# Local attention layers: table products from PSUM, own buffers for rotated q and k, feed-forward per batch, new order

## The chip, the core and the metric

The kernel runs on one core of a Trainium2 chip. A core has TensorE (PE: matmuls and transposes, results into PSUM), VectorE (DVE), ScalarE (ACT: activation functions, copies out of PSUM), GpSimd (POOL: elementwise work on SBUF) and SyncE (SP: here it starts the DMA transfers). They run side by side, each through its own instructions in their written order, and wait for each other on semaphores. The metric is the device time of one execution in microseconds (us); lower is better.

## What is computed

x has 8 batches of 256 tokens of 128 numbers. It passes a state space block, a cross attention block and six layers of local attention with feed-forward; after each of the three comes x = layernorm(x + block(x)). Only the six layers matter here. For one layer (16 heads of 64 numbers, windows of 32 tokens, 341 hidden numbers):

```python
def attn_layer(x, Wqkv, qs, ksc, Wo):
    q, k, v = split(x @ Wqkv)                  # per head
    q, k = l2norm(q) * qs, l2norm(k) * ksc
    q = q * cos * scale + rotate_half(q) * sin * scale
    k = k * cos / scale + rotate_half(k) * sin / scale
    # each window of 32 queries sees its own and the previous 32 keys
    attn = softmax(where(mask, -inf, q @ k.T * 8))
    return (attn @ v) @ Wo

def ffn_layer(x, g, bln, W1, b1, W2, b2):
    a, gate = split((layernorm(x) * g + bln) @ W1 + b1)
    return a * gelu(gate) @ W2 + b2

for i in range(6):
    x = attn_layer(shift_tokens(x), ...) + x
    x = ffn_layer(shift_tokens(x), ...) + x
```

shift_tokens moves the upper 64 columns down by one token.

## The kernel before

Three blocks follow each other: state_space_block, cross_attention_block, window_layers. Only window_layers (and the packing of its weights) is touched. The whole x lies in SBUF (xall, 16 tiles of 128 tokens by 128). A batch is two tiles, t = 0 and 1. There are ITERS = 6 x 8 = 48 iterations i (layer i // 8, batch i % 8), and two slots in each. The loop over i is the same on every engine; the order inside a slot is written out by hand in a function slot(i, t, stages) of each engine. A slot works on up to four tiles at once, in four stages:

- A, unit u: the token tile is transposed (transpose_tokens, L1314, in the slot before), six projections of 512 columns (project, L1399) go through the two PSUM banks psA: four for q and k, two for v. ScalarE copies the first four to qkraw (L1125) and squares them (L1162). VectorE multiplies qkraw with the cosine and sine tables into m12 (L1250, one product of 128x2048 each for q and k) and sums the squares (L1268). GpSimd makes the scaled table (L1054), adds the two halves in place in m12 (rotate, L1035) and multiplies with 1/norm into qkr (scale, L1041). ScalarE copies v (L1110); SyncE moves it into V96.
- B, the unit before (v): q and k are transposed (L1393, into psA again) and copied (L1132), then for two groups g of 8 heads: scores (L1344 for the mask, L1350), maximum and subtraction (L1220, L1225), exponentials (L1118), denominators (L1229, L1231), normalisation on GpSimd (L1029), transposes of the probabilities (L1362), copies (L1101) and the product with v (times_v, L1383; group 1 one slot later). psS, psP and psO are one buffer each.
- C, the unit before that (wu): the output projection (L1453), the residual x1 (L1263), the shift of x1 into xsC by DMA (L986, L987), layer norm statistics (L1271, L1274), the normalised tile hatC (L1284). GpSimd adds the bias b2 to x1 (x1b, L1070).
- D, the unit three back (du), one tile a slot: hatC is transposed (L1410), scaled (xnT, L1143), multiplied with both halves of W1 (w1, L1424, tokens in the rows, 341 columns each), the bias added (L1240), GELU (L1165, with a table load before it and one after it, L1166), the product a x gelu on GpSimd (hh, L1062), three transposes (L1467), two copies (hT, L1177 and L1178), the product with W2 (L1484) and the residual addition into xall (L1288).

ScalarE holds one table set of functions at a time: GELU is in another than exponential and logarithm. The weights of a layer (f_W) come in eight shares, one per iteration, all sizes packed by column (W_QKV, W_O, W_1, ...), L1009. The helper weights_here waits for the share that holds a column; A_full[n] and A_free[n] mark the fills of psA: 0 to 3 for q and k, 4 to 7 for their transposes, 8 and 9 for v.

## Time and profile before

| what | value |
|---|---|
| median of 3 runs | 2977.41 us (2975.38 to 2978.07) |
| the profiled execution, its own time | 2978.97 us |
| its span (first to last instruction) | 2977.2 us |
| mean granted TensorE clock | 0.977 |
| busy, share of the span: TensorE | 2639.6 us, 89% |
| VectorE | 2064.9 us, 69% |
| ScalarE | 1929.3 us, 65% |
| GpSimd | 1649.6 us, 55% |
| window layers, first to last L1054 | 831.8 to 2896.9 us |

A share of the span is an average over all three blocks. What one slot of the window layers costs is read from a stretch of the trace: the busy times of one slot, TensorE's rows in order of time, and the chain of work, which goes back from the last instruction to what released it, step by step. A matmul row's end overlaps the start of the next, so the distance of two starts tells the cost, not the duration.

### The profile page before, as it was taken

How to read it: one execution, taken by the hardware profiler on the slowest of the kernel's cores; microseconds unless marked ns; L12 is line 12 of the kernel's file. 1: busy time of each engine (PE TensorE's matmuls, PEld its weight loads, DVE VectorE, ACT ScalarE, POOL GpSimd, SP SyncE). 2: the span in 40 equal slices, each digit the busy share in tenths (PEclk: the TensorE clock that was granted, in tenths of full speed). 3: DMA queues.
4: the chain of work that ended last, by engine and by line, in shares of the span. 5: the costliest groups of instructions: out<-in, count | busy, mean ns of one | idle time of the engine just before them, and what ended most of it. 6: DMA issues, size and time to landing. Idle time of an engine off the chain costs nothing.

```text
span 2977.2 us, 64423 instructions
## 1 busy us (share of the span) xinstructions
PE 2639.6 (89%) x23097; PEld 1760.7 (59%) x23097; DVE 2064.9 (69%) x3311; ACT 1929.3 (65%) x3411; POOL 1649.6 (55%) x1188
## 2 busy tenths in 40 slices
PE   5787788999979999999999999999999999999995
PEld 2343345777746666666666666666666666666664
DVE  6898995555556767677676777767677676767764
ACT  3233232333357778787777878777787877778784
POOL 1342441000047777676777767677776777767672
PEclk9998999999989999999999999999999999999997
DMA  2000001000011121212112121211212121121211
GB/s 100 1 0 0 1 0 47 0 0 0 0 34 47 41 54 46 56 39 56 46 39 56 46 56 39 56 46 39 56 46 56 39 54 48 39 56 46 54 41 33
DMA packets 86713, 112.65 MB, mean 38 GB/s; under 512 B 60944, under 2 KB 62096, under 8 KB 85904
## 3 DMA queue, kind: packets, MB, share of 16 engines
q1 hardware_dynamic: 86672, 112.20, 14.3%
q8 instruction: 14, 0.23, 0.0%
q14 instruction: 27, 0.22, 0.0%
HBM read 29.28 MB, written 1.05 MB: 10 GB/s over the span
## 4 chain that ended last, share of the span: by engine, by line
ACT 26%; DVE 13%; POOL 12%; PE 9%; issue 5%; DMA 5%; SPq 1%; POOLq 0%; DVEq 0%; ACTq 0%
POOL f_qkr L1041 10%; ACT f_sq L1162 6%; DVE f_den L1229 5%; DMA f_xsC<-f_x 4%; ACT L1165 4%; ACT L1166 3%; ACT f_qT L1132 3%; ACT f_kT L1132 3%; DVE f_ssq L1268 3%; ACT f_Pr L1118 3%; PE f_psA L1399 2%; POOL f_Pr L1029 2%; PE f_psA L1393 2%; PE f_psO L1383 2%; ACT f_oT L1114 2%
## 5 line engine op out<-in xcount | busy, mean ns | idle before, releaser
L1035 POOL TENSOR_TENSOR f_m<-f_m 128x1024 f32<-128x1024 f32 x192 | 637.8, 3342 | 241.9 <-DVE f_m L1250 241.9
L1250 DVE TENSOR_TENSOR f_m<-f_qkraw,f_tab 128x2048 f32<-128x2048 f32 x192 | 433.5, 2299 | 480.7 <-POOL f_tab L1054 470.7
L1399 PE MATMUL f_psA<-f_W,f_xT 128*128 (+1 forms) x1152 | 605.8, 622 | 12.9 <-issue 8.1
L1029 POOL TENSOR_TENSOR f_Pr<-f_Pr,f_rden 128x384 f32<-128x384 f32 x384 | 310.1, 828 | 372.3 <-DVE f_rden L1231 372.3
L1041 POOL TENSOR_TENSOR f_qkr<-f_m,f_rn 128x1024 f32<-128x1024 f32 x192 | 361.0, 1901 | 0.9 <-DVE f_rn L1281 0.9
L208 POOL TENSOR_TENSOR m_HC<-m_Hs,m_Ct 128x512 f32<-128x512 f32 x128 | 163.8, 1279 | 299.6 <-DVE m_Hs L349 299.6
L1362 PE MATMUL f_psP<-ident,f_Pr 128*96 128x128 f32 x1536 | 238.1, 278 | 100.6 <-POOL f_Pr L1029 65.8
L1362 PEld LDWEIGHTS f_psP<-ident,f_Pr 128*96 128x96 f32 x1536 | 156.4, 127 | 267.8 <-POOL f_Pr L1029 149.6
L1125 ACT ACTIVATE f_qkraw<-f_psA 128x512 f32<-128x512 f32 x384 | 228.7, 596 | 110.0 <-PE f_psA L1399 110.0
L1101 ACT ACTIVATE f_PT<-f_psP 96x512 f32<-96x512 f32 x384 | 228.5, 595 | 84.4 <-PE f_psP L1362 79.3
L1383 PEld LDWEIGHTS f_psO<-f_PT,f_V 96*64 96x64 f32 x6144 | 217.7, 138 | 100.9 <-issue 89.3
L1054 POOL TENSOR_TENSOR f_tab<-f_base_tab,f_W 128x256 f32<-128x256 f32 x96 | 69.8, 727 | 368.0 <-DVE f_maskb L1215 368.0
L1383 PE MATMUL f_psO<-f_PT,f_V 96*64 96x64 f32 x6144 | 257.6, 230 | 0.0
L1229 DVE TENSOR_REDUCE f_den<-f_Pr 128x8 f32<-128x768 f32 x192 | 179.8, 937 | 107.5 <-ACT f_Pr L1118 107.3
L1350 PE MATMUL f_psS<-f_kT,f_qT 64*64 64x96 f32 x6144 | 244.0, 249 | 0.0
L1350 PEld LDWEIGHTS f_psS<-f_kT,f_qT 64*64 64x64 f32 x6144 | 207.8, 133 | 60.9 <-issue 60.9
L1399 PEld LDWEIGHTS f_psA<-f_W,f_xT 128*128 128x128 f32 x1152 | 181.7, 191 | 96.8 <-issue 61.8
L263 ACT ACTIVATE m_psD<-m_psD,m_negA 128x512 f32<-128x512 f32 x128 | 84.7, 662 | 227.1 <-PE m_psD L423 227.1
L1268 DVE TENSOR_REDUCE f_ssq<-f_sq 128x32 f32<-128x2048 f32 x96 | 218.5, 2276 | 0.0
L1453 PEld LDWEIGHTS f_psO<-f_W,f_oT 128*128 128x128 f32 x1536 | 187.8, 193 | 45.5 <-issue 45.4
L1393 PE MATMUL f_psA<-ident,f_qkr 128*128 128x128 f32 x1536 | 206.8, 278 | 7.3 <-POOL f_qkr L1041 1.5
L1393 PEld LDWEIGHTS f_psA<-ident,f_qkr 128*128 128x128 f32 x1536 | 173.6, 142 | 45.5 <-ACT f_qT L1132 20.9
(172 smaller groups left out, 5160.1 us busy)
## 6 DMA issues: line engine op xcount, KB each, us to landing
f_V<-f_Vt SPq DMA_DIRECT2D x96, 384.0 KB, 4.3
f_V<-f_Vt SPq DMA_DIRECT2D x96, 256.0 KB, 3.6
f_W<-in_f_W SPq DMA_DIRECT2D x48, 381.5 KB, 3.8
f_V<-f_Vt SPq DMA_DIRECT2D x48, 128.0 KB, 4.6
f_xsA<-xall SPq DMA_DIRECT2D x97, 32.0 KB
f_xsA<-xall SPq DMA_DIRECT2D x97, 31.8 KB
f_xsC<-f_x SPq DMA_DIRECT2D x96, 32.0 KB
f_xsC<-f_x SPq DMA_DIRECT2D x96, 31.8 KB
```

Source lines behind the costliest of these rows:

```text
L1029: pool.tensor_tensor(pv, pv, rv.unsqueeze(3).broadcast_to([P, 2, 2, KEYS]), ALU.mult).then_inc(Pr_ready[g][j], 1)
L1035: pool.tensor_tensor(mv[:, 0], mv[:, 0], mv[:, 1, :, ::-1, :], ALU.add).then_inc(rot_done[j], 1)
L1041: pool.tensor_tensor(qkr[:, j * INNER:(j + 1) * INNER].rearrange("p (h d) -> p h d", d=DH), m12[:, j, 0, :].rearrange("p (h d) -> p h d", ...
L1125: act.activation(qkraw[:, n * 512:(n + 1) * 512], psA[n % 2][:, :], ACT.Copy).then_inc(A_free[n], 1)
L1229: dve.tensor_reduce(den[:, g, :], Pr[:, g, :, :], axis=AX.X, op=ALU.add).then_inc(den_done[g], 1)
L1250: dve.tensor_tensor(m12[:, j, :, :].rearrange("p m (h d) -> p m h d", d=DH), rv.unsqueeze(1).broadcast_to([P, 2, H, DH]), tab[:, t, j, :, ...
L1268: dve.tensor_reduce(ssq[:, :], sq[:, :].rearrange("p (h d) -> p h d", d=DH), axis=AX.X, op=ALU.add).then_inc(ssq_ready, 1)
L1350: ins = pe.matmul(S4[half * HQ:(half + 1) * HQ, par, c, :], qT[r, q, 4 * g + c, k0:k0 + HQ], kT[r, q, 4 * g + c, k0:k0 + KEYS], start=Fals ...
L1362: ins = pe.transpose(psP[0:KEYS, n, :], Pr[:, g, (h % 2) * 4 + h // 2, :], ident[:, :])
L1383: ins = pe.matmul(psO[(h % 2) * DH:(h % 2) * DH + DH, h // 2, half * HQ:(half + 1) * HQ], V96[:, tile, half, hh_ * DH:(hh_ + 1) * DH], PT[ ...
L1393: ins = pe.transpose(p[:, c * P:(c + 1) * P], qkr[:, col:col + P], ident[:, :])
L1399: pe.matmul(psA[n % 2][:, :], xT[:, t, :], weights(i, W_QKV + n * 512, 512), start=True, stop=True).then_inc(A_full[n_fill], 1)
```

## The change

- The table products read the projections from PSUM, four of 128x1024 instead of two of 128x2048 (table_products). Each frees its bank. The squares are taken from PSUM too, 512 columns at a time (square). qkraw goes. The sum of squares stands right behind the products.
- rotate writes into qkr, which now has a buffer for each t, as two instructions of 512 for each of q and k; scale works in place there. The table of a slot is made in the slot before (scaled_tables).
- The feed-forward runs once per batch, over both tiles (256 tokens): stage D in slots with t = 0 and stage E in slots with t = 1. hatC of both tiles is transposed into xnT (256 columns), W1 is the stationary operand and comes as its own transfer f_W1 into its own buffer (once per iteration, waiting for h01_ready and h2_ready), its bias a column. So the hidden numbers lie in the partitions, in three pieces (FC = 128, 128, 85), GELU takes the bias from its own instruction, the gated product is one VectorE instruction a piece (gated), and no transposes, hidden copies or bias additions remain. Table loads for GELU come once per two slots. w2 runs for both tiles in E.
- x1 + b2 goes straight into xall; the residual addition takes both tiles at once.
- The order on every engine is new: see the slots below. times_v alternates between the two heads of a pair.

```diff
@@ GpSimd @@
+            def rotate(u, t, j):
+                pool.wait_ge(A_free[2 * j + 1], u + 1)
+                at_least(pool, A_full[7], u - 1)
                 mv = m12[:, j, :, :].rearrange("p m (h two d) -> p m h two d", two=2, d=DH // 2)
-                pool.tensor_tensor(mv[:, 0], mv[:, 0], mv[:, 1, :, ::-1, :], ALU.add).then_inc(rot_done[j], 1)
+                qv = qkr[:, t, j * INNER:(j + 1) * INNER].rearrange("p (h two d) -> p h two d", two=2, d=DH // 2)
+                pool.tensor_tensor(qv[:, :, 0, :], mv[:, 0, :, 0, :], mv[:, 1, :, 1, :], ALU.add)
+                pool.tensor_tensor(qv[:, :, 1, :], mv[:, 0, :, 1, :], mv[:, 1, :, 0, :], ALU.add).then_inc(rot_done[j], 1)
...
                 if "A" in stages:
+                    rotate(u, t, 0)
+                    rotate(u, t, 1)
+                    scaled_tables(u + 1, i + t, 1 - t)
...
@@ ScalarE @@
-                    act.activation(qkraw[:, n * 512:(n + 1) * 512], psA[n % 2][:, :], ACT.Copy).then_inc(A_free[n], 1)
+                    act.activation(sq[:, n * 512:(n + 1) * 512], psA[n % 2][:, :], ACT.Square).then_inc(squared[n], 1)
...
                 if "A" in stages:
+                    square(0)
+                if "D" in stages:
...
+                    act.activation(xnT[:, :], psD[0][:, 0:T2], ACT.Identity, bias=weights(i - 2, W_LN + 1, 1), scale=weights(i - 2, W_LN, 1)).then_inc(xnT_ready, 1)
+                if "A" in stages:
+                    square(1)
                 if "C" in stages:
                     evacuate_probs(1, 0)
...
                 if "C" in stages:
                     evacuate_out(1)
                 if "B" in stages:
+                    evacuate_qk(1)
+                if "D" in stages:
+                    at_least(act, h01_ready, (i - 2) * 2)
+                    at_least(act, h2_ready, i - 2)
+                    for c in range(3):
+                        src, j = bank_of(c)
+                        if c != 1:
+                            act.wait_ge(gate_full[j], i - 1)
+                        act.activation(ge[0:FC[c], c, :], src[0:FC[c], :], ACT.Gelu, bias=bias_col(3 + c)[0:FC[c], :]).then_inc(ge_ready, 1)
+                    act.preload_act_table_set(LN_EXP)
+                if "B" in stages:
                     evacuate_qk(2)
                     evacuate_qk(3)
-                if "A" in stages:
-                    act.wait_ge(A_free[3], u + 1)
-                    act.activation(sq[:, :], qkraw[:, :], ACT.Square).then_inc(sq_ready, 1)
...
                     exponentials(0)
...
+                    evacuate_tokens(u + 1, 1 - t)
+                    evacuate_v(0)
+                if "B" in stages:
+                    evacuate_probs(0, 0)
+                    exponentials(1)
+                    evacuate_probs(0, 1)
...
+                if "A" in stages:
+                    evacuate_v(1)
                 if "B" in stages:
                     evacuate_out(0)
@@ VectorE @@
+                def gated(c):
+                    src, j = bank_of(c)
+                    if c != 1:
+                        dve.wait_ge(a_full[j], i - 1)
+                    dve.scalar_tensor_tensor(out=hT[0:FC[c], c, :], in0=src[0:FC[c], :], scalar=bias_col(c)[0:FC[c], :],
+                                             in1=ge[0:FC[c], c, :], op0=ALU.add, op1=ALU.mult).then_inc((h01_ready, h01_ready, h2_ready)[c], 1)
+                def table_products(n):
+                    j = n // 2
...
+                    dve.wait_ge(squared[n], u + 1)
+                    half = slice((n % 2) * 512, (n % 2) * 512 + 512)
+                    dve.tensor_tensor(m12[:, j, :, half].rearrange("p m (h d) -> p m h d", d=DH),
+                                      psA[n % 2][:, :].rearrange("p (h d) -> p h d", d=DH).unsqueeze(1).broadcast_to([P, 2, H // 2, DH]),
+                                      tab[:, t, j, :, :].unsqueeze(2).broadcast_to([P, 2, H // 2, DH]), ALU.mult).then_inc(A_free[n], 1)
...
+                    for n in range(4):
+                        table_products(n)
+                    dve.wait_ge(squared[3], u + 1)
+                    dve.tensor_reduce(ssq[:, :], sq[:, :].rearrange("p (h d) -> p h d", d=DH), axis=AX.X, op=ALU.add).then_inc(ssq_ready, 1)
+                if "E" in stages:
+                    dve.wait_ge(ge_ready, (i - 1) * 3)
+                    gated(2)
                 if "B" in stages:
                     less_maximum(v, 0)
...
+                if "E" in stages:
+                    gated(0)
+                    gated(1)
...
                 if "B" in stages:
                     denominators(v, 1)
+                if "E" in stages:
+                    dve.wait_ge(w2_full, i - 1)
+                    dve.wait_ge(x1b_ready, (i - 1) * 2)
+                    alone(dve, passed)
+                    dve.tensor_tensor(tiles_of(i - 2), psD[0][:, T2:2 * T2].rearrange("p (t d) -> p t d", d=D), tiles_of(i - 2), ALU.add).then_inc(x2_done, 2)
@@ TensorE, times_v @@
-                    for n in range(4):
-                        h = 4 * j + n
-                        hh_ = 8 * g + h
-                        for half in range(2):
+                    for pair in range(2):
+                        for half, n in ((0, 2 * pair), (0, 2 * pair + 1), (1, 2 * pair), (1, 2 * pair + 1)):
...
+                def w1(n, c, full):
+                    ins = pe.matmul(bank_of(c)[0][0:FC[c], :], W1[:, n * FF + c * P:n * FF + c * P + FC[c]], xnT[:, :], start=True, stop=True)
@@ SyncE @@
+                if "E" in stages and not (isinstance(i, int) and i > ITERS):
+                    sp.wait_ge(h01_ready, (i - 1) * 2)
+                    sp.wait_ge(h2_ready, i - 1)
+                    load_up_projection(i - 1)
```

TensorE's new order in a slot (D and E only in theirs): project 0; D: transposes of hatC; project 1; D: w1 of the gate's third piece, E: w1 of the value's first two; transpose_probs(1, 0); project 2, 3; transpose_probs(1, 1); times_v(1, 0); transpose_qk(0); times_v(1, 1); transpose_qk(1); E: w1 of the value's third piece, D: w1 of the gate's first two; transpose_qk(2); scores(0); transpose_qk(3); output projection; scores(1); transpose_tokens; project 4; transpose_probs(0, 0); project 5; transpose_probs(0, 1); times_v(0, 0); E: w2; times_v(0, 1). GpSimd's: rotate twice, scaled_tables, probabilities of group 0, x1 + b2, probabilities of group 1, scale twice. SyncE in E: the shift of x1, then load_up_projection, then the V copies.

## Rows read from the trace of the kernel before

**Rows 1.** One line's answer: durations ns min/median/max, first and last start.

```profile
L1054 POOL TENSOR_TENSOR f_tab<-f_base_tab,f_W x96: 722/726/737, 831.8 to 2896.9; 128x256 f32<-128x256 f32 x96
```

**Rows 2.** Busy times of one slot: PE, PEld, DVE, ACT, POOL, then PEclk.

```profile
2006.47:2028.22 21.75, 20.32 (x209) 13.65 (x208) 15.31 (x21) 17.12 (x30) 15.50 (x11) 1.00 0.14 36
```

**Rows 3.** The chain of work in this slot: start, us, what.

```profile
2001.96 3.77 POOL f_qkr L1041 x2
...
2006.47 0.60 ACT f_qT L1132
...
2009.02 1.79 ACT f_sq L1162
2010.83 1.28 ACT L1165
...
2013.92 0.85 ACT f_Pr L1118
...
2016.90 3.45 DMA f_xsC<-f_x
```

**Rows 4.** Waits from 1450 to 2850: us in total, times, longest.

```profile
DVE f_m L1250 <- POOL f_tab L1054: 316.5, 64, 5.0
```

**Rows 5.** TensorE in order of time: start, us, what, idle before.

```profile
2006.70 0.74 PE L1424 MATMUL f_psD<-f_W,f_xnT 128*128 x2
2007.28 1.03 PE L1393 MATMUL f_psA<-ident,f_qkr 128*128 128x128 f32 x8
2008.15 0.74 PE L1424 MATMUL f_psD<-f_W,f_xnT 128*128 x2
2009.12 0.48 PE L1344 MATMUL f_psS<-f_maskb,f_identb 128*128 128x384 bf16 x2 [0.23 <-issue]
2009.54 1.27 PE L1350 MATMUL f_psS<-f_kT,f_qT 64*64 64x96 f32 x32
2010.74 1.12 PE L1399 MATMUL f_psA<-f_W,f_xT 128*128 x2
2011.70 1.95 PE L1453 MATMUL f_psO<-f_W,f_oT 128*128 x16
2013.78 0.50 PE L1344 MATMUL f_psS<-f_maskb,f_identb 128*128 128x384 bf16 x2
...
2015.41 1.12 PE L1399 MATMUL f_psA<-f_W,f_xT 128*128 x2
2017.19 0.64 PE L1362 MATMUL f_psP<-ident,f_Pr 128*96 128x128 f32 x4 [0.65 <-POOL f_Pr L1029]
2017.66 0.49 PE L1467 MATMUL f_psD<-ident,f_hh 128*128 128x128 f32 x3
2017.99 0.27 PE L1314 MATMUL f_psD<-ident,f_xsA 128*128 128x128 f32 x1
2018.60 0.61 PE L1362 MATMUL f_psP<-ident,f_Pr 128*96 128x128 f32 x4 [0.34 <-ACT f_PT L1101]
2019.15 0.73 PE L1383 MATMUL f_psO<-f_PT,f_V 96*64 96x64 f32 x16
2019.81 0.94 PE L1484 MATMUL f_psD<-f_W,f_hT 128*128 x6
2020.67 0.73 PE L1383 MATMUL f_psO<-f_PT,f_V 96*64 96x64 f32 x16
```

**Rows 6.** Four lines' answers: durations ns min/median/max, first and last start.

```profile
L1225 DVE TENSOR_TENSOR f_Pr<-f_psS,f_mx x192: 957/958/959, 862.6 to 2930.4; 128x768 f32<-128x768 f32 x192
...
L1250 DVE TENSOR_TENSOR f_m<-f_qkraw,f_tab x192: 2283/2291/4307, 841.3 to 2899.9; 128x2048 f32<-128x2048 f32 x192
...
L1035 POOL TENSOR_TENSOR f_m<-f_m x192: 2346/2378/4353, 843.6 to 2904.4; 128x1024 f32<-128x1024 f32 x192
...
L1284 DVE TENSOR_SCALAR f_hatC<-f_xsC,f_momC,f_rstdC x96: 296/965/967, 891.8 to 2951.4; 128x128 f32<-128x128 f32 x96
```

**Rows 7.** DMA issues: KB each, median us from issue to landing.

```profile
f_W<-in_f_W SPq DMA_DIRECT2D x48, 381.5 KB, 3.8
```

More of the change, by code:

```diff
@@ L798, in window_layers @@
     GH = H // 2
+    FC = [min(P, FF - c * P) for c in range(3)]
+    T2 = TPB * P
     with ExitStack() as ctx:
@@ L870, in window_layers @@
         kprev_ready = sem("f_kprev_ready")
-        m12_done = [sem(f"f_m12_done{j}") for j in range(2)]
-        sq_ready = sem("f_sq_ready")
+        squared = [sem(f"f_squared{n}") for n in range(4)]
         ssq_ready = sem("f_ssq_ready")
@@ L898, in window_layers @@
         hatC_ready = sem("f_hatC_ready")
+        w1_loaded = sem("f_w1_loaded")
         xn_full = sem("f_xn_full")
         xnT_ready = sem("f_xnT_ready")
-        ga_full = [sem("f_a_full"), sem("f_gate_full")]
-        ga_ready = [sem("f_a_ready"), sem("f_gate_ready")]
+        gate_full = [sem(f"f_gate_full{j}") for j in range(2)]
+        a_full = [sem(f"f_a_full{j}") for j in range(2)]
         ge_ready = sem("f_ge_ready")
-        hh_ready = sem("f_hh_ready")
-        hT_full = sem("f_hT_full")
-        hT_ready = sem("f_hT_ready")
+        h01_ready = sem("f_h01_ready")
+        h2_ready = sem("f_h2_ready")
         w2_full = sem("f_w2_full")
@@ L1481, in slot @@
                     p = psD[0]
-                    for c in range(3):
-                        n = min(P, FF - c * P)
-                        ins = pe.matmul(p[:, 0:D], hT[0:n, c, :], weights(di, W_2 + c * D, D)[0:n, :], start=(c == 0), stop=(c == 2))
+                    for tt in range(TPB):
+                        for c in range(3):
+                            ins = pe.matmul(p[:, T2 + tt * D:T2 + (tt + 1) * D], hT[0:FC[c], c, tt * P:(tt + 1) * P],
+                                            weights(i - 2, W_2 + c * D, D)[0:FC[c], :], start=(c == 0), stop=(c == 2))
                     ins.then_inc(w2_full, 1)
@@ L1541, in host_layout @@
     w["f_W"] = pack.reshape(P, DEPTH, B, SHARE)
+    up_proj = np.zeros((P, DEPTH, W1_COLS), f)
+    for l in range(DEPTH):
+        up_proj[:, l, 0:2 * FF] = x["L0_ffn_W1"][l]
+        for n in range(2):
+            for c in range(3):
+                m = min(P, FF - c * P)
+                up_proj[0:m, l, 2 * FF + 3 * n + c] = x["L0_ffn_b1"][l][n * FF + c * P:n * FF + c * P + m]
+    w["f_W1"] = up_proj
     half = np.arange(0, DH, 2, dtype=f)
```

296 lines of the change are left out of this document (134 added, 162 removed).

## The prediction

> **What bounds the kernel now.** I read the first and last start of a line that runs once per slot, then the busy times of one slot, then the chain of work, then TensorE's rows in order of time, then the waits. Only the window layers change. Their line 1054 runs 96 times from 831.8 to 2896.9 us [rows 1]: 95 slot pitches of 2065.1 / 95 = 21.74 us, which is 2065 of the 2977.2 us of the span. So the question is what one slot costs.
>
> In one slot TensorE is busy 20.32 us of 21.75, ScalarE 17.12, GpSimd 15.50, VectorE 15.31, at a granted clock of 1.00, the upper level, 2.4 GHz [rows 2]. TensorE is nearly full, but it doesn't set the pitch: the chain [rows 3] goes in a circle of latencies: GpSimd scales q and k (3.77 us for both), TensorE transposes, ScalarE copies (0.60), squares (1.79), loads a table (1.28), does the GELU, loads the other table, does the exponentials (0.85); then come denominators, the shift DMA (3.45) and probabilities, and GpSimd scales again. VectorE meanwhile waits 316.5 us over 64 slots, 4.9 us in each, for the table that GpSimd only makes after the scaling [rows 4].
>
> How much of TensorE's slot is work? I take starts, not durations, since a pipelined row's end overlaps the next [rows 5]. Gate and value matmul (341 columns each) have a pitch of 0.58 (2006.70 to 2007.28). The second ends about 2008.73 and the scores start at 2009.12: 0.39 idle. The output projection ends at 2013.65, the next at 2013.78: 0.13. A projection has a pitch of 0.96 (2010.74 to 2011.70), so the one of 2015.41 ends at 2016.37 and the next work starts at 2017.19: 0.82. The token transpose ends at 2018.26, the next starts at 2018.60: 0.34. That is 1.68 us of idle time between groups, and 21.74 - 1.68 = 20.06 us in which TensorE works or issues. Some 0.3 of it is issue at the slot's head. This is the floor that the change can reach if it only takes waits away.
>
> **The change, part by part.** I walk the new order with these pitches, from P, the start of a slot's first projection.
>
> *TensorE's own work.* Feed-forward per pair of slots, before: four matmuls of 0.58, twice the three hidden transposes of 0.33 (2017.66 to 2017.99), two transposes of the normalised tile, so 0.11 each, twice w2 of 0.86 (2019.81 to 2020.67): 2.32 + 0.66 + 0.22 + 1.72 = 4.92. After: six matmuls of 256 columns, estimated 0.58 x 256/341 = 0.435 each, 2.61; 0.22; no hidden transposes; 1.72: 4.55. So -0.18 us a slot. The times_v matmuls alternate the two column halves of the array. Their 16 records take 0.66 us (2019.15 to 2019.81), 41 ns each. The scores, which already alternate, take 1.20 for 32 records of 96 columns (2009.54 to 2010.74), 37 ns each. So the gain for the 64 records of a slot lies between 0 and, at 64/96 of 37 ns, 64 x 16 ns = 1.0 us. No loss, as it is the same matmuls on the same banks. I take 0.15 us, near the no-gain end (64 x 4 ns would be 0.25), because no record in the rows is shorter than 37 ns. Sum: 20.06 - 0.18 - 0.15 = 19.73.
>
> *ScalarE.* The four raw copies become four squares of the same size (0.60 each [rows 3]; no cost against before), and the 1.79 us square of 2048 goes. GELU once per two slots: one pair of table loads (2 x 1.28 us) less per pair; three GELUs of 256 columns at about 0.35 (0.60 for 512 and 0.85 for 768 differ by 0.25) for two of 341; the hidden copies go. So 1.79 and 1.28 leave each slot, and 17.12 falls to some 13.5 us. None of it is slot time by itself, since TensorE is the floor; it shortens the circle.
>
> *VectorE.* The two products of 2048 outputs become four of 1024 that read PSUM. No row has that form. The nearest is 128x768 from PSUM in 957 ns [rows 6]; with 256 elements more at its own rate (1334 ns for 1280 more in the 2291 ns of the long form, 1.04 each) it is 1.22 us. Low end: the long form halved, 1.15. High end: the 2.29 us of the long form, if a short one cost as much. I take 1.22, since 768 is the nearest size and also from PSUM. The four bias additions of 341 a pair become three gated products of 256. VectorE stays near 16 us.
>
> The Trainium skill, page "VectorE: DVE Perf Modes", section on the TRN2 errata, gives 120 cycles plus one per element from PSUM against 58 from SBUF at 0.96 GHz, and warns of many small tiles; by it a product would be an estimated 1.19 us. The rows above give 1.22, so it agrees and speaks against the split only by some 0.1 us a product.
>
> *GpSimd.* The rotation takes 2346 ns at least and 4353 at most [rows 6]. The first of a slot's two is the long one, by the 2.0 us that VectorE's second table product, with two SBUF inputs, still runs beside it. The new product has one input in PSUM, so I take 2.4 us for both halves of each rotation, now two instructions, 5.0 a slot. The hidden product goes. GpSimd falls from 15.5 to some 13 us. The table is now made a slot ahead, so VectorE's 4.9 us wait goes, and what is late next for it is the bank, below.
>
> *The banks, the new wait.* A psA bank is now held through projection, square and product: 0.96 + 0.60 + 1.22 = 2.8 us. The third projection waits for the first product (P+2.85). Queued behind it on TensorE are probability transposes, times_v and the q/k transposes. What stands before it (two projections, in D 0.22 of transposes and one w1 matmul, in E two w1 matmuls, then four transposes, 0.47 as at 2017.19) ends at P+2.95 in a D slot and P+3.2 in an E slot: covered. The fourth waits for the second product, P+4.0: 0.1 us late in D. The q transposes need the third product (P+5.9), the k transposes the fourth (P+7.05 to 7.3) and TensorE comes there at P+5.95 and P+7.0 to 7.15: 0.05 to 0.15 late. If these covers were gone, the four products would stand end to end, below.
>
> *The middle.* In D, ScalarE goes from the first k copy (P+8.25) through load, three GELUs and load to P+11.8, then the second q and k copies to P+12.95; TensorE, with w1 (0.87), transposes, scores 1.62 and the output projection 1.95, comes to the second scores at P+12.9. Level. First scores end at P+10.5, maximum and subtraction 1.95, free at 12.55. Second scores end at 14.6, tokens and projection 15.8, first probabilities 16.3 (GpSimd's first part is ready at 15.8), projection 17.25, second 17.7, times_v 18.3; the last copy of probabilities stands behind the second exponentials (P+17.8) and is done at 18.4, so 0.1 to 0.15 idle, and the slot ends at P+19.0. E has w2 for both tiles (1.72) and no transposes: 20.2. Mean 19.6, plus 0.2 for issue at the slot's head. This agrees with 19.73 plus about 0.1 of new waits. I take **19.8 us a slot**.
>
> *The circle.* Scales end at P+5.45 and are next wanted at P+7.0: from the k scale over the k transposes, w1, scores, output projection, scores, maximum, exponentials, denominators, probabilities and scales 3.77 I get 17.5 us, 2.3 under the slot. This is the slack of my forecast.
>
> *Moved queues.* SyncE: the load of W1 (344 KB, the nearest row is the 381.5 KB of f_W at 3.8 us [rows 7]) waits for the gated products (P+17.3 in E) and lands by P+21.8, with 0.7 allowed for issue, against TensorE's first gate matmul at P+20.2+2.06 = P+22.3. Behind it in the queue stand the V copies (wanted 8 us later) and the weight share: free. The second V copy on ScalarE now stands behind the normalisation's statistics, whose shift DMA takes 3.45 us [rows 3]: done at P+19.5 against the second projection at P+19.9. Head and tail: the last feed-forward runs for two tiles in one piece, I add 2 us (I allow -3 to +6).
>
> **Sum.** 95 x (21.74 - 19.8) = 184 us. From the profiled execution's own 2978.97 us (span 2977.2 and 1.8 around it): 2978.97 - 184 + 2 = 2797; the median of the runs, 2977.41, is 1.6 lower: **2795 us**.
>
> **Rivals.**
> *A, late in D.* The normalised tile of the second half now stands behind the residual addition, which waits for w2. That line takes 965 ns where 296 is its least [rows 6]: it sits out a GpSimd instruction. In E it comes at P+20.15; from P+20.6 GpSimd scales, 1.9 us a piece. If w2 ends 0.5 us later than I think, the tile is done at P+22.5, and the transposes, wanted at P+21.1, lose 1.4 us; W1 landing 1 us late costs the same place. 0.7 a slot, at most 0.95: 20.5 to 20.75, 2861 to 2885 us. For it: only 0.4 us of slack. Against: in the profile it slips in between two GpSimd instructions. The Trainium skill, page "SBUF — State Buffer", section "Who interferes with whom", says that whichever of the two starts first holds the shared pair for the whole instruction; the 965 ns agree.
> *B, the circle still binds.* If handovers that I counted at nothing come to 3.5 us or more in the circle (its some twenty steps, ScalarE's long order with the GELU block in D), the slot is about 21.2: 2978.97 - 95 x 0.54 = 2928. Against: it needs all of the 2.3 us of slack first. It covers 20.8 to 21.6.
> *C, slower: the bank ring.* After the fourth product a slot still has 12.4 us of TensorE's work. With x per product the slot is 1.65 + 4x + 12.4, which passes 21.74 from x = 1.92 us. At 2.29, the high end, it is 23.2: 2978.97 + 95 x 1.46 = 3118. For it: no row has the broadcast product from PSUM. Against: the 957 ns.
> *D, faster.* Alternation gives 0.6 or more and nothing new waits: 19.2, 2738 us.
> *E.* The change does its parts but nothing moves: within 0.2%, about what a measurement of this kernel tells from no change.
>
> **Chances.** Forecast (19.4 to 20.3 a slot, 2757 to 2843): 0.54. D: 0.08. A: 0.18. B: 0.10. E: 0.02. C and other slower outcomes: 0.08. So faster 0.90, same 0.02, slower 0.08. The range has the forecast, most of D and A: 2735 to 2885, leaving 0.2 out.
>
> **What would show it.** Line 1250's answer after should be four products of 1.2 us a slot, and no wait on the table; the rotation without its 4.3 us form; TensorE's gaps of 0.82 and 0.34 gone, no wait over 0.2 us except before the D transposes (A) or the w1 of D (W1's DMA). A mean slot over 20.4 with a chain through GpSimd's scales is B, one through VectorE's products C. I am wrong first where an order on an engine makes it wait for something that I placed too early, since a slot has nine places with under 0.5 us of slack.

## The result and the profile after

The changed kernel takes a median of 2874.47 us (2873.04 to 2876.50, 4 runs), the kernel before 2976.39 us in the same comparison. The ratio is 0.9658, 95% interval 0.9641 to 0.9675: 102 us or 3.4% less. The forecast was 2795 us, with a range of 2735 to 2885. So the direction is right and the time lies in the range, but the gain is 102 us where 182 were forecast. The time also lies outside the prediction's own forecast interval, 2757 to 2843, in the part of the range that it gave to rival A.

From the page of after: its head, the chain that ended last, one group and one DMA issue (the load of W1):

```profile
span 2873.1 us, 64292 instructions
...
PE 2609.1 (91%) x23001; PEld 1748.1 (61%) x23001; DVE 2044.3 (71%) x3407; ACT 1632.8 (57%) x3027; POOL 1411.9 (49%) x1285
...
issue 29%; POOL 24%; PE 10%; DVE 5%; ACT 1%; POOLq 1%; DMA 0%; DVEq 0%; SPq 0%; ACTq 0%
...
L1264 DVE TENSOR_TENSOR f_m<-f_psA,f_tab 128x1024 f32<-128x1024 f32 x384 | 452.7, 1220 | 243.7 <-ACT f_sq L1142 243.7
...
f_W<-in_f_W SPq DMA_DIRECT2D x48, 344.0 KB, 3.0
```

Slots now come in pairs, one with t = 0 (D: transposes the normalised tiles, GELU) and one with t = 1 (E: the product with W2). Below, P is again the start of a slot's first projection. The busy times of an E slot and the D slot behind it, columns as in [rows 2]:

```profile
2000.91:2021.76 20.85, 20.56 (x216) 14.25 (x212) 15.56 (x24) 12.48 (x25) 14.08 (x14) 1.00 0.22 56
2021.76:2042.26 20.50, 19.32 (x201) 12.90 (x202) 14.64 (x21) 15.87 (x30) 11.90 (x12) 1.00 0.23 58
```

E 20.85 and D 20.50, so 20.68 us a slot, where [rows 2] had 21.75 and the forecast 19.8. In E, TensorE is busy 20.56 of 20.85 us: full. In D it is busy 19.32 of 20.50. The granted clock is 1.00 in both, 2.4 GHz, as before.

The waits of after, from 1450 to 2750 us (62 slots), to be laid beside [rows 4]:

```profile
DVE f_m L1264 <- ACT f_sq L1142: 153.3, 125, 1.8
...
PEld f_psA L1433 <- DVE f_m L1264: 33.0, 64, 0.8
...
PE f_psS L1374 <- ACT f_kT L1149: 24.0, 32, 0.8
```

The 316.5 us wait for the table is gone. VectorE now waits for squares. TensorE waits for a product that frees its bank (PEld is its weight load: the wait stands there), once in each D slot for the copy of k (0.75) and once in each D slot for xnT (0.33). The gaps of 0.82 and 0.34 of [rows 5] are gone, as forecast. TensorE's order, first in the E slot, then in the D slot, columns as in [rows 5]:

```profile
2000.91 1.98 PE L1433 MATMUL f_psA<-f_W,f_xT 128*128 x4
2002.73 1.03 PE L1437 MATMUL f_psD<-f_xnT,f_W 128*128 128x256 f32 x4
...
2004.14 2.25 PE L1433 MATMUL f_psA<-f_W,f_xT 128*128 x4
2006.24 0.60 PE L1396 MATMUL f_psP<-ident,f_Pr 128*96 128x128 f32 x4
...
2007.38 0.66 PE L1427 MATMUL f_psA<-ident,f_qkr 128*128 128x128 f32 x4
...
2021.76 1.12 PE L1433 MATMUL f_psA<-f_W,f_xT 128*128 x2 [0.21 <-issue]
...
2024.29 0.63 PE L1437 MATMUL f_psD<-f_xnT,f_W 128*85 128x256 f32 x2 [0.33 <-ACT f_xnT L1157]
...
2025.20 2.06 PE L1433 MATMUL f_psA<-f_W,f_xT 128*128 x4
2027.10 0.60 PE L1396 MATMUL f_psP<-ident,f_Pr 128*96 128x128 f32 x4
...
2028.33 0.63 PE L1427 MATMUL f_psA<-ident,f_qkr 128*128 128x128 f32 x4
...
2036.11 0.48 PE L1374 MATMUL f_psS<-f_maskb,f_identb 128*128 128x384 bf16 x2 [0.75 <-ACT f_kT L1149]
```

And ScalarE in the same slot (start, us, what, idle before), with the cause of that 0.75:

```profile
2022.91 0.60 ACT L1142 ACTIVATE f_sq<-f_psA 128x512 f32<-128x512 f32 x1 [0.72 <-PE f_psA L1433]
...
2030.19 0.60 ACT L1149 ACTIVATE f_kT<-f_psA 128x512 f32<-128x512 f32 x1
2031.13 1.28 ACT L1183 ACT_TABLE_LOAD   x1 [0.34 <-PE f_psD L1437]
2032.42 1.20 ACT L1183 ACTIVATE f_ge<-f_psD,f_W 128x256 f32<-128x256 f32 x3
2033.63 1.28 ACT L1184 ACT_TABLE_LOAD   x1
2034.93 0.60 ACT L1149 ACTIVATE f_qT<-f_psA 128x512 f32<-128x512 f32 x1
2035.42 0.59 ACT L1149 ACTIVATE f_kT<-f_psA 128x512 f32<-128x512 f32 x1
```

The load has line 1183, that of the first GELU: the program has no load of its own there, and the row shows the load itself waiting for the gate matmuls. VectorE's first two products in this slot:

```profile
2023.64 2.35 DVE L1264 TENSOR_TENSOR f_m<-f_psA,f_tab 128x1024 f32<-128x1024 f32 x2 [1.32 <-ACT f_sq L1142]
```

### The profile page after: what moved, and what is told of

Its sections match the earlier page's. It is cut to its first block, busy times and chain, and to the rows that moved or that the text cites. A ratio compares the mean times of both kernels' runs of the same rounds, so it can differ in the third digit from the quotient of the medians.

```text
span 2873.1 us, 64292 instructions
## 1 busy us (share of the span) xinstructions
PE 2609.1 (91%) x23001; PEld 1748.1 (61%) x23001; DVE 2044.3 (71%) x3407; ACT 1632.8 (57%) x3027; POOL 1411.9 (49%) x1285
## 4 chain that ended last, share of the span: by engine, by line
issue 29%; POOL 24%; PE 10%; DVE 5%; ACT 1%; POOLq 1%; DMA 0%; DVEq 0%; SPq 0%; ACTq 0%
POOL f_qkr L1068 8%; POOL f_qkr L1075 5%; POOL f_Pr L1050 5%; POOL f_qkr L1067 4%; DVE f_m L1264 4%; PE f_psA L1433 3%; PE f_psD L1527 2%; POOL f_tab L1058 2%; PE f_psO L1417 2%; PE f_psP L1396 2%; ACT f_sq L1142 1%; POOL xall L1089 1%; POOLq L1058 0%; POOLq L1089 0%; PE f_psD L1437 0%
## 5 line engine op out<-in xcount | busy, mean ns | idle before, releaser
L1264 DVE TENSOR_TENSOR f_m<-f_psA,f_tab 128x1024 f32<-128x1024 f32 x384 | 452.7, 1220 | 243.7 <-ACT f_sq L1142 243.7
L1075 POOL TENSOR_TENSOR f_qkr<-f_qkr,f_rn 128x1024 f32<-128x1024 f32 x192 | 361.1, 1900 | 0.3 <-DVE f_rn L1293 0.3
L1142 ACT ACTIVATE f_sq<-f_psA 128x512 f32<-128x512 f32 x384 | 229.0, 596 | 144.7 <-PE f_psA L1433 138.5
L1396 PEld LDWEIGHTS f_psP<-ident,f_Pr 128*96 128x96 f32 x1536 | 166.1, 127 | 219.9 <-POOL f_Pr L1050 152.6
L1067 POOL TENSOR_TENSOR f_qkr<-f_m 128x512 f32<-128x512 f32 x192 | 244.7, 1275 | 55.3 <-DVE f_m L1264 55.3
L1417 PE MATMUL f_psO<-f_PT,f_V 96*64 96x64 f32 x6144 | 264.4, 229 | 3.4
L1232 DVE TENSOR_REDUCE f_mx<-f_psS 128x8 f32<-128x768 f32 x192 | 179.7, 936 | 122.3 <-PE f_psS L1380 122.3
L1417 PEld LDWEIGHTS f_psO<-f_PT,f_V 96*64 96x64 f32 x6144 | 211.2, 138 | 67.4 <-issue 51.4
L1427 PE MATMUL f_psA<-ident,f_qkr 128*128 128x128 f32 x1536 | 246.0, 283 | 2.3 <-DVE f_m L1264 1.4
L1068 POOL TENSOR_TENSOR f_qkr<-f_m 128x512 f32<-128x512 f32 x192 | 244.5, 1273 | 0.0
```

The source lines that it names most:

```text
L1067: pool.tensor_tensor(qv[:, :, 0, :], mv[:, 0, :, 0, :], mv[:, 1, :, 1, :], ALU.add)
L1068: pool.tensor_tensor(qv[:, :, 1, :], mv[:, 0, :, 1, :], mv[:, 1, :, 0, :], ALU.add).then_inc(rot_done[j], 1)
L1075: pool.tensor_tensor(qv, qv, rn[:, j * H:(j + 1) * H].unsqueeze(2).broadcast_to([P, H, DH]), ALU.mult).then_inc(qkr_ready[j], 1)
L1142: act.activation(sq[:, n * 512:(n + 1) * 512], psA[n % 2][:, :], ACT.Square).then_inc(squared[n], 1)
L1264: dve.tensor_tensor(m12[:, j, :, half].rearrange("p m (h d) -> p m h d", d=DH), psA[n % 2][:, :].rearrange("p (h d) -> p h d", d=DH).unsqu ...
L1396: ins = pe.transpose(psP[0:KEYS, n, :], Pr[:, g, (h % 2) * 4 + h // 2, :], ident[:, :])
```

## The experiments

The theory: a slot of after is TensorE's own order plus two dependent waits: the bank ring (a projection fills a bank, ScalarE squares it, VectorE's product frees it for the next projection) and the late GELU load. The rival, B of the prediction: the circle through GpSimd's scales still binds. It had a case. The page's chain gives GpSimd 24%, its largest named part, and the mean slot of 20.68 is over the 20.4 that the prediction named as B's sign. All differences below are of medians, against 2874.47 of after or 2977 of before; the intervals are those of the ratio to before.

### Is it the circle? (slack, circle)

slack puts one more GpSimd instruction ahead of the scales:

```diff
                 if "A" in stages:
+                    at_least(pool, scratched, u)
+                    flat = base_tab[:, :, :, :, :].rearrange("p t a b d -> p (t a b d)")
+                    pool.tensor_tensor(scratch[:, :], flat, flat, ALU.mult).then_inc(scratched, 1)
                     scale(u, t, 0)
```

> The changed kernel with one more GpSimd instruction a slot, 128x512 into a buffer that nobody reads, between the second group's probabilities and the scales (about 1.28 us, as line 208), the table left where it was. Theory 1 (TensorE's order, the circle has 2.07 us of slack at the first k transposes and 2.7 at the first q transposes): 2874 us within 6. Rival (the circle through GpSimd sets the slot): 95 x 1.28 = 122 us more, 2996 us.

Measured: 2876.64 us, ratio 0.9658 (0.9642 to 0.9674), 2 us from after. GpSimd in order of time in this kernel:

```profile
2004.01 1.62 POOL L1052 TENSOR_TENSOR f_Pr<-f_Pr,f_rden 128x384 f32<-128x384 f32 x2 [2.20 <-DVE f_rden L1248]
2005.60 1.04 POOL L1097 TENSOR_TENSOR f_scratch<-f_base_tab 128x512 f32<-128x512 f32 x1
2006.59 3.76 POOL L1077 TENSOR_TENSOR f_qkr<-f_qkr,f_rn 128x1024 f32<-128x1024 f32 x2
```

The instruction takes 1.04 us, not the 1.28 expected. The scales start 1.0 us later in both slots (P+2.56 in E instead of P+1.57), and the time doesn't move; a binding circle would have made it some 95 us more. Rival B falls. The 24% of the chain are a trap of reading: the chain is one path of releases, with 29% of "issue" on it, for which the profile names no cause. That GpSimd stands on it doesn't say that the time follows GpSimd.

circle makes the table of the next slot just ahead of the scales, 0.72 us in the circle:

```diff
                     rotate(u, t, 1)
-                    scaled_tables(u + 1, i + t, 1 - t)
...
                 if "A" in stages:
+                    scaled_tables(u + 1, i + t, 1 - t)
                     scale(u, t, 0)
```

> The changed kernel with one move: GpSimd makes the scaled table (0.73 us) right ahead of the two scales instead of behind the rotations, so that it lies in the circle scales, transposes, scores, exponentials, probabilities, scales. Theory 1 (TensorE's order sets the slot, the circle has over 2 us of slack): no change, 2874 us within 5. Rival (the circle through GpSimd sets it, as the chain of work of the profile after suggests with its 24% GpSimd): 95 x 0.73 = 69 us more, 2943 us.

Measured: 2898.94 us, ratio 0.9742 (0.9725 to 0.9758), 24 us more than after (the profiled execution, 2891.10 us, is 16 more than that of after): neither number. VectorE's row, then TensorE's, in an E slot with P = 2011.02:

```profile
2013.34 2.36 DVE L1264 TENSOR_TENSOR f_m<-f_psA,f_tab 128x1024 f32<-128x1024 f32 x2 [2.19 <-POOL f_tab L1058]
```

```profile
2014.62 2.26 PE L1433 MATMUL f_psA<-f_W,f_xT 128*128 x4 [0.32 <-DVE f_m L1264]
```

The table has a second user, the next slot's first product. In E slots VectorE now waits 2.19 us for the table, where in after it waits 1.82 for the square: the product starts at P+2.32 instead of P+1.96, the bank is held 0.36 longer, and the whole E slot takes 21.21 us instead of 20.85, while D stays at 20.50. 0.36 x 47.5 pairs is 17 us, the lengthening of the profiled execution. So the experiment moved two things at once, and slack, with nothing hanging on its result, decides about the circle. But it shows by accident that in E slots the first product's start counts in full: the bank ring binds there.

### The late table load (gelu_early)

```diff
                     evacuate_probs(1, 1)
+                if "D" in stages:
+                    act.preload_act_table_set("gelu_and_others")
                 if "B" in stages:
                     evacuate_qk(0)
```

> The changed kernel with the table for GELU loaded in D slots ahead of the first q copy, instead of behind the wait for the gate matmuls. Theory 1: TensorE's wait of 0.75 us in each D slot ahead of the second scores is ScalarE's two loads and three GELUs ahead of the last k copy; it goes: 47 x 0.75 = 35 us less, 2839 us. Rival: the load only makes the first q and k copies late by about 0.7 us, which TensorE then waits for ahead of the first scores: 0 to 10 us less.

Measured: 2840.63 us, ratio 0.9539 (0.9523 to 0.9555), 34 us less than after, as expected. The load now begins where ScalarE of after sat idle for 0.62 us ahead of the q copy. That copy comes 0.71 later in the slot, but TensorE's first scores only 0.07, so the rival's wait doesn't appear. ScalarE, and then TensorE at the second scores of the D slot:

```profile
2013.30 1.28 ACT L1171 ACT_TABLE_LOAD   x1
2014.60 0.60 ACT L1149 ACTIVATE f_qT<-f_psA 128x512 f32<-128x512 f32 x1
```

```profile
2020.19 0.48 PE L1376 MATMUL f_psS<-f_maskb,f_identb 128*128 128x384 bf16 x2
```

No wait stands at the scores. The D slot takes 19.77 us (2006.66 to 2026.43) instead of 20.50: 0.73 x 47.5 pairs is 35 us. The 0.75 is settled.

### The xnT wait and the bank ring (w1_late, swap)

w1_late moves the gate matmul that waits for xnT behind four transposes; swap lets the last transposes of probabilities go ahead of the fourth projection:

```diff
@@ w1_late @@
-                if "D" in stages:
-                    pe.wait_ge(w1_loaded, (i - 1) * 16)
-                    pe.wait_ge(xnT_ready, i - 1)
-                    w1(1, 2, gate_full)
...
                     transpose_probs(1, 0)
+                if "D" in stages:
+                    pe.wait_ge(w1_loaded, (i - 1) * 16)
+                    pe.wait_ge(xnT_ready, i - 1)
+                    w1(1, 2, gate_full)
@@ swap @@
                     project(2)
-                    project(3)
                 if "C" in stages:
                     transpose_probs(1, 1)
+                if "A" in stages:
+                    project(3)
+                if "C" in stages:
                     times_v(1, 0)
```

In swap the square of the fourth projection on ScalarE moves behind the copy of those probabilities too.

> The changed kernel with the first gate matmul of a D slot behind the transposes of probabilities instead of ahead of them. Theory 1: the 0.33 us that TensorE waits there for xnT is covered: 47 x 0.33 = 16 us less, 2859 us. Rival: the third projection, next in order, is bound by the product that frees its bank, and the time comes back there: 0.

> The changed kernel with the second transposes of probabilities ahead of the fourth projection instead of behind it (and the copy ahead of the fourth square on ScalarE). Theory 1: the bank ring (projection 1.14, square 0.60, two products 2.4, handovers) holds the fourth projection back to 4.4 us after the slot's start in both slots, whatever stands before it; work moved into that wait is free: 0.25 us a slot, 24 us less, 2850 us. Rival: the fourth product then comes later by as much and the k transposes wait: 0 within 5 us.

Measured: w1_late 2875.96 us, ratio 0.9657 (0.9640 to 0.9673): nothing. swap 2880.39 us, ratio 0.9674 (0.9657 to 0.9691): 6 us more. TensorE in order of time in w1_late:

```profile
2026.97 0.63 PE L1437 MATMUL f_psD<-f_xnT,f_W 128*85 128x256 f32 x2
2027.68 2.25 PE L1433 MATMUL f_psA<-f_W,f_xT 128*128 x4
2029.77 0.60 PE L1396 MATMUL f_psP<-ident,f_Pr 128*96 128x128 f32 x4
```

and in swap:

```profile
2016.33 0.63 PE L1429 MATMUL f_psA<-ident,f_qkr 128*128 128x128 f32 x4 [0.20 <-DVE f_m L1266]
```

In w1_late the xnT wait is gone (no bracket at 2026.97), but the pair of projections takes 2.25 instead of 2.06: its second one waits for the bank, and the next group starts at P+5.34 (2024.43 to 2029.77), as in after (2021.76 to 2027.10, 5.34). The 0.33 us lay in the shadow of the ring. In swap the projection no longer waits, but the next user of the same banks does, the q transposes: they start at P+6.46 in E, as in after (6.47), and in D the k transposes start 0.15 later (P+7.89 instead of P+7.74), 7 us over 47.5 pairs. Neither reordering shortened this part; the ring of projection, square and product sets it.

### Does interleaving cover a copy? (tv_together)

```diff
                     times_v(1, 0)
+                    times_v(1, 1)
                 if "B" in stages:
                     pe.wait_ge(qkr_ready[0], v + 1)
                     transpose_qk(0)
-                if "C" in stages:
-                    times_v(1, 1)
```

> The changed kernel with the two times_v pieces of group 1 behind each other again and then the first q and k transposes. Theory 1: alternating between the two kinds costs TensorE 0.25 us a slot (2.31 us for the four pieces, against 2.06 in the kernel before): 24 us less, 2850 us. Rival: the k transposes then wait for the fourth table product and nothing is gained: 0 within 5 us.

Measured: 2915.87 us, ratio 0.9800 (0.9784 to 0.9817), 41 us more. Neither theory had that. TensorE, one D slot and the following E slot:

```profile
2019.45 0.48 PE L1374 MATMUL f_psS<-f_maskb,f_identb 128*128 128x384 bf16 x2 [0.84 <-ACT f_kT L1149]
...
2031.44 1.49 PE L1417 MATMUL f_psO<-f_PT,f_V 96*64 96x64 f32 x32
...
2035.23 0.49 PE L1374 MATMUL f_psS<-f_maskb,f_identb 128*128 128x384 bf16 x2 [0.37 <-issue]
```

The q transposes of the E slot start at P+7.27 (2025.59 to 2032.86) instead of P+6.47, so ScalarE's copies come later (it sits idle 1.36 us ahead of a q copy), and the first scores now wait in E (the row names no releaser; the k copy ahead of them ends at 2035.13), the second still in D. The halves of times_v cover ScalarE's copies on both sides. The expectation counted switches on TensorE and left out what each piece hides.

### Alternating column halves (no_alternation, before_alt)

```diff
-                    for pair in range(2):
-                        for half, n in ((0, 2 * pair), (0, 2 * pair + 1), (1, 2 * pair), (1, 2 * pair + 1)):
-                            h = 4 * j + n
-                            hh_ = 8 * g + h
+                    for n in range(4):
+                        h = 4 * j + n
+                        hh_ = 8 * g + h
+                        for half in range(2):
```

before_alt makes the opposite edit in the kernel before.

> The changed kernel with the matmuls of times_v in the order of before (both halves of a head, then the next head). Theory 1: a piece of 16 records costs 0.66 us again instead of 0.61, four a slot: 95 x 0.18 = 17 us more, 2891 us, less where a wait takes it. Rival: the order of the records is no cause, the piece stays at 0.61: 0 within 5 us.

> The kernel before, with the matmuls of times_v alternating between the two heads of a pair as in the changed kernel. Taken back in the changed kernel this cost 15 us. Theory 1: in the kernel before, the circle sets the slot and TensorE's shorter pieces end in longer waits, except for the last pieces of a slot that stand between the probabilities and the next unit's transposes: 0 to 5 us less. Rival: the work of an engine that is 89% busy counts anywhere: 15 us less.

Measured: no_alternation 2889.14 us, ratio 0.9708 (0.9691 to 0.9724), 15 us more than after. before_alt 2978.06 us over 10 runs, ratio 1.000 (0.999 to 1.001): nothing. TensorE in no_alternation:

```profile
2016.48 0.73 PE L1417 MATMUL f_psO<-f_PT,f_V 96*64 96x64 f32 x16
2017.14 0.66 PE L1427 MATMUL f_psA<-ident,f_qkr 128*128 128x128 f32 x4
```

Sixteen records take 0.66 us, with the alternation 0.62 (in w1_late 2030.30 to 2030.92); 64 records give 0.16 to 0.2 us a slot, 15 to 19 us. The forecast's 0.15 was right. The same edit is worth 15 us where TensorE sets the pitch, and nothing where it doesn't.

### Own buffers and products from PSUM, apart (before_own, after_shared)

before_own gives the kernel before the own qkr buffers, the rotation in two instructions and the table a slot ahead; its products still read qkraw in SBUF, and no longer wait for the scales. after_shared takes the own buffers away from after:

```diff
@@ before_own, GpSimd and VectorE @@
+                qv = qkr[:, t, j * INNER:(j + 1) * INNER].rearrange("p (h two d) -> p h two d", two=2, d=DH // 2)
+                pool.tensor_tensor(qv[:, :, 0, :], mv[:, 0, :, 0, :], mv[:, 1, :, 1, :], ALU.add)
+                pool.tensor_tensor(qv[:, :, 1, :], mv[:, 0, :, 1, :], mv[:, 1, :, 0, :], ALU.add).then_inc(rot_done[j], 1)
...
-                        dve.wait_ge(qkr_ready[1], u)
+                        at_least(dve, rot_done[j], u)
@@ after_shared @@
+                pool.tensor_tensor(mv[:, 0], mv[:, 0], mv[:, 1, :, ::-1, :], ALU.add).then_inc(rot_done[j], 1)
...
-                        at_least(dve, rot_done[j], u)
+                        at_least(dve, qkr_ready[j], u)
```

> The kernel before, with the changed kernel's own buffers for rotated q and k (two rotations of 512 each into qkr, scale in place) and the table made a slot ahead. VectorE's products then no longer wait 4.9 us for the scales of the unit before. Theory 1: the chain of work doesn't pass through the products but through copies, squares and table loads on ScalarE, so the 4.9 us are no cost: 0 to 20 us less (the 0.73 us of the table leave GpSimd, nothing else on the chain). Rival (the products' wait is the cost that the change removes): over 60 us less.

> The changed kernel with the rotation in place in m12 again and the scales from there to qkr, so that VectorE's products of a unit wait for the scales of the unit before. In the trace of the changed kernel the q scale ends 1.5 us behind the start of the first product in E slots and 0.45 us behind it in D slots. Theory 1: the bank ring is late by that much: about 1.0 us a slot, 95 us more, 2970 us. Rival: the ring has room or VectorE makes it up: under 30 us more.

Measured: before_own 3189.30 us, ratio 1.0712 (1.0695 to 1.0730), **212 us more** than before; both theories had a gain. after_shared 2980.06 us over 10 runs, ratio 1.0007 (0.9998 to 1.0017): 106 us more than after, so the whole gain is gone, as expected. GpSimd in before_own:

```profile
2003.83 5.81 POOL L1052 TENSOR_TENSOR f_qkr<-f_qkr,f_rn 128x1024 f32<-128x1024 f32 x2
2009.60 3.32 POOL L1044 TENSOR_TENSOR f_qkr<-f_m 128x512 f32<-128x512 f32 x1
```

VectorE there:

```profile
2004.01 7.77 DVE L1250 TENSOR_TENSOR f_m<-f_qkraw,f_tab 128x2048 f32<-128x2048 f32 x2 [0.65 <-ACT f_qkraw L1126]
```

and TensorE:

```profile
2009.69 1.09 PE L1393 MATMUL f_psA<-ident,f_qkr 128*128 128x128 f32 x8 [2.13 <-POOL f_qkr L1052]
```

Freed from its wait, the product starts 0.2 us behind the scales and runs against them. The two take turns, each held for the whole of the other's instruction: scale 1.9, product 2.3, scale 1.9, product 2.3 from 2003.83 on gives 2009.9 and 2012.2, and the rows end at 2009.64 and 2011.78; then the rotation is held until the second product ends (3.32 instead of 1.27). So two products take 7.77 us, where two of 2.29 [rows 6] are 4.6, two scales 5.81 where [rows 3] has 3.77, and TensorE waits 2.13 us for q. The Trainium skill says this in "SBUF — State Buffer", section "Who interferes with whom": a VectorE instruction with two SBUF inputs contends with a GpSimd one that reads SBUF, one with at most one SBUF input (outside the two-port modes) doesn't. Both halves agree with rows here: in after the same product with one input in PSUM runs beside the same scales. GpSimd, then VectorE, of after:

```profile
2002.48 3.76 POOL L1075 TENSOR_TENSOR f_qkr<-f_qkr,f_rn 128x1024 f32<-128x1024 f32 x2
```

```profile
2002.87 2.35 DVE L1264 TENSOR_TENSOR f_m<-f_psA,f_tab 128x1024 f32<-128x1024 f32 x2 [1.82 <-ACT f_sq L1142]
```

3.76 and 2.35 us at the same time, neither longer than alone: all 384 products of after take between 1212 and 1226 ns. after_shared shows the other half, a wait of VectorE (waits, 1450 to 2750 us):

```profile
DVE f_m L1262 <- POOL f_qkr L1073: 158.7, 60, 3.4
```

In E slots the product waits 3.4 us for the scales, where in after it waits 1.8 for the square: the bank is held 1.6 us longer and the ring stretches by as much. In these two kernels neither part gains anything without the other: the buffer lets the product start while the scales run, and PSUM as its source makes that harmless.

### The circle of before, tried alone (before_exp)

```diff
-                    act.activation(ge[:, :], ga[:, 1, :], ACT.Gelu).then_inc(ge_ready, 1)
+                    act.activation(ge[:, :], ga[:, 1, :], ACT.Exp).then_inc(ge_ready, 1)
```

> The kernel before, with the GELU replaced by an exponential, so that no table is loaded in a slot (the feed-forward computes a x exp(gate) instead of a x gelu(gate)). This takes two loads of 1.28 us out of ScalarE's part of the circle and leaves everything else. Theory 1 (the kernel before is set by the circle, over a floor of TensorE's own work of 20.06 us a slot): the slot falls by 1.7 us, where the floor stops it, or by less if another wait comes first; 95 x 1.7 = 161 us, 2816 us; between 2816 and 2870. Rival (TensorE already sets the slot): 0 within 10 us.

Measured: 2958.07 us, ratio 0.9935 (0.9918 to 0.9951): 19 us less, where 161 less was the largest expected. VectorE in this kernel, and then two waits of ScalarE for VectorE (1450 to 2750 us):

```profile
2016.15 4.49 DVE L1250 TENSOR_TENSOR f_m<-f_qkraw,f_tab 128x2048 f32<-128x2048 f32 x2 [4.95 <-POOL f_tab L1054]
2020.56 0.93 DVE L1240 TENSOR_TENSOR f_ga<-f_psD,f_W 128x341 f32<-128x341 f32 x2
```

```profile
ACT f_Pr L1118 <- DVE f_Pr L1225: 31.7, 60, 0.6
...
ACT f_ge L1165 <- DVE f_ga L1240: 29.4, 60, 0.6
```

Only the load ahead of the activation vanished; the one behind it, 1.28 us, is still made. Of the 1.28 us that ScalarE won only 0.2 a slot reached the time; the rest ended in waits for VectorE, since a second circle of nearly the same length runs beside the first: scales, table, both long products, bias additions, maximum, subtraction, exponentials. [rows 3] shows only the one that came last. So before could only become faster by shortening both, and the change has neither the 1.79 us square nor the 4.9 us wait for the table.

### The best order (best)

gelu_early, w1_late and swap together. With swap's order the load stands behind the fourth square:

```diff
                     evacuate_probs(1, 1)
+                if "A" in stages:
+                    square(3)
+                if "D" in stages:
+                    act.preload_act_table_set("gelu_and_others")
```

> The changed kernel with the early load of the GELU table, the first gate matmul behind the transposes of probabilities in D, and the swap of run swap. Theory 1 (bank ring and ScalarE's GELU block are the two waits): 34 us from the load, 24 from the swap, some 5 more because the moved gate matmul stands in the ring's wait: 2811 us. Rival (only the load counts): 2841 us.

Measured: 2832.34 us, ratio 0.9510 (0.9494 to 0.9526), 42 us less than after and 8 less than gelu_early: nearer to the sum in which the reorderings add nothing (2841) than to the full one (2811). Alone they brought 0 and 6 us more, together with the early load 8 less, so their effects don't add up. It is the fastest version of all. Its slots are 19.64 and 20.82 us (2001.50, 2021.14 and 2041.96):

```profile
2007.98 0.63 PE L1431 MATMUL f_psA<-ident,f_qkr 128*128 128x128 f32 x4 [0.19 <-DVE f_m L1268]
```

Even here the ring shows, 0.19 us at the q transposes.

## Why the prediction was right, and its size wrong

**What bounds before.** That waits and not TensorE's work set the pitch was read rightly: before_alt takes work from TensorE and gains nothing. But the circle of [rows 3] doesn't set it alone: before_exp shows a twin over VectorE. The prediction wasn't hurt, because the change shortens both.

**The prices.** The product: 1.22 taken, 1220 ns measured; rival C (from 1.92 us) never came near. Rotation: 2.4 for a half pair, measured 1.28 + 1.28 with starts 1.24 apart, 2.5. Alternation: 0.15 taken, 15 us of 95 slots measured. GELU: 0.35 each for three, 1.20 measured for all, 0.15 more. GpSimd: 14.08 and 11.90 busy, mean 12.99, "some 13" taken. ScalarE: mean 14.18, 13.5 taken. W1's load: 3.0 us, no wait for it anywhere.

**The bank ring, mis-sized.** The prediction let the square start 0.96 us after its projection starts, and the product 0.60 later, P+1.6. But 0.96 is the pitch, the distance to the next start on the same engine, not the end of the work. The rows: projection at 2021.76, square at 2022.91, product at 2023.64, so P+1.88, in E P+1.96. The Trainium skill, "TensorE: Matmul & The Clock Gate", sections "Single matmul latency" and "Back-to-back issue gap", has one formula for a matmul from start to end and another, shorter one for the distance of two starts; the difference is an estimated 0.16 us by its figures. The rows agree: a projection has a pitch of 0.96 and is over after 1.12. The first two products end at P+4.2 to P+4.3 instead of P+4.0; the group behind the fourth projection starts at P+5.34 in D and P+5.33 in E; and the q transposes, forecast at P+5.95, start at P+6.57 and P+6.47. The 0.2 allowed for issue isn't part of this: the rows have it ahead of P (0.21 at 2021.76). In D the forecast counted 0.1 for the ring, the rows have 0.33 (the wait for xnT, which w1_late shows to be the ring's) and 0.1 ahead of the q transposes: 0.3 to 0.4 is new. In E the forecast's own terms come to P+6.2 (P+3.2, two projections 1.92, transposes 0.47, times_v 0.62). The third and fourth projection take 2.10 to the next start, where the first two take 1.82, so the ring costs 0.2 to 0.3 there.

**Small pitches.** The rest of E's error, 20.85 against 20.4 (20.2 and 0.2), lies in TensorE's own work. The four groups of q and k transposes have pitches of 0.59, 0.49, 0.46 and 0.50, together 2.04, where [rows 5] give 1.74 (eight matmuls in 0.87), and the four transposes of probabilities 2.09 instead of 1.88. The output projection (1.78 instead of 1.95) and w2 (1.53 instead of 1.72) give part of that back.

**"The middle. Level." This step failed.** It put the load at P+8.25, right behind the first k copy. It is at P+9.37 (2031.13). Of these 1.12 us, 0.78 is the k copy itself, which ends at P+9.03, since TensorE's transposes come late; 0.34 is ScalarE idle, because the load stands behind the wait of the GELU that needs it, the wait for the gate matmuls. The prediction's own sentence took for granted that the load could start early; the diff has a load by hand behind the GELUs only. With the GELUs' extra 0.15 the second k copy ends at P+14.25 instead of P+12.95. TensorE is late too, but less: it would have been there at P+13.6 instead of P+12.9, and waits 0.75. gelu_early takes the load out of this stretch, and 34 us come back. In D the sum is 0.3 to 0.4 for the ring, 0.75 for the load and some 0.15 in small pitches: 20.50 against 19.2.

**The sum.** D 1.30 and E 0.45 late make 0.875 a slot. Times 95 that is 83 us of the 79.5 that were missing; the other 3.5 us are what head and tail did better than the 2 that were added (where exactly isn't shown).

**Rival A** (the tile late in D): its numbers, 20.5 to 20.75 a slot, hold the measured 20.68, but its mechanism didn't happen. Line 1314, the tile of the second half, takes 0.64 from 2021.68 on and is over at 2022.32; the transposes start right behind the first projection, at 2022.71, and don't wait. xnT is 0.33 late in D, and w1_late shows that this costs nothing. So that the range holds the time is in part luck: without A's share it would have ended at 2843. Being right about a number says nothing about the reason.

**Rival B** (the circle) had 0.10 and fell by slack. The sign that the prediction named for it, a mean slot over 20.4 with a chain through GpSimd's scales, appeared all the same, so it was no sign. The 2.3 us of slack forecast are borne out down to the 1.0 that slack used up; how much more there is wasn't measured.

**What stays open.** A kernel in which product and square read one bank side by side, which would take 0.6 us out of the ring, wasn't tried. So the ring is shown by where waits move (w1_late, swap) and by lengthening it (circle, after_shared), not by taking it away, and why the small transposes take longer in the new order isn't shown. Nor was it measured what the feed-forward per batch and the new order are worth by themselves: after_shared has both, but not the own buffers, and gains nothing.

## What to carry to other kernels

Walk a new order with two kinds of numbers: pitches between starts for what stands on the same engine, start to end and the handover (0.03 and 0.13 us in the rows above) for whoever waits for a result. A table load that the program doesn't place stands behind the wait of its first user, so place it by hand where the engine sits idle. Before a wait is removed, ask what the freed instruction will now run beside: own buffers, with the table a slot ahead, cost 212 us with products from two SBUF inputs, and without them the kernel with products from PSUM had no gain at all.

## What the runs showed of the hardware

- VectorE products with two SBUF inputs and GpSimd instructions on SBUF take strict turns, and both pay: 3.9 us instead of 2.29 for a product, up to 3.9 instead of 1.9 for a scale, 3.32 instead of 1.27 for a rotation. With one input in PSUM neither pays.
- A switch of ScalarE's table costs its 1.28 us and nothing more: the load of 2033.63 is followed by a copy at 2034.93, that of gelu_early at 2013.30 by one at 2014.60. The Trainium skill, "ScalarE: Activation LUTs", section "What ACT_TABLE_LOAD costs", has the same load but another 1.38 us of draining, 2.66 in all; here the measurement decides, 1.30.
- Matmuls of 64 columns that change the column half of the array with each one take 0.62 us for 16, those that change it with every second one 0.66.
